# A fused attention and mixture-of-experts kernel: the query and key factors on VectorE, and the stack rows stored and loaded for all 512 tokens at once

## The chip, the cores and the metric

The kernel runs on one core of a Trainium2 chip. A core has TensorE (matrix products, and transposes as products with an identity matrix), VectorE, ScalarE and GpSimd for everything elementwise, and SyncE, which here only issues DMAs; the DMA engines move data between the chip's DRAM and the on-chip memory SBUF (128 partitions). Products are written to PSUM, eight banks of 2 KB per partition. In views of the profile the engines are PE (PEld for its loads of weights), DVE, ACT, POOL and SP. The metric is the device time of one execution in microseconds; lower is better.

## The reference

The input is 16 sequences of 512 tokens with 256 channels. Two blocks follow one another, each with a layer norm ahead of it and a residual around it:

```
x = x + attention_1(layernorm(x))      # 16 heads of 16, causal
x = x + ffn(layernorm(x))

attention_1:  q, k, v = x @ Wq.T, x @ Wk.T, x @ Wv.T, in 16 heads of 16
              q = layernorm(q, gq, bq);  k = layernorm(k, gk, bk)      # over the 16 channels of a head
              out = softmax(causal(q k^T)) v @ Wo.T + bo

ffn:          x = x + attention_2(rmsnorm(x))        # latent keys and values, rotary, 16 heads of 64
              x = x + moe(rmsnorm(x))                # 8 routed experts (top 2) and a shared one
```

`gq, bq, gk, bk` are the factors (gains) and offsets of the norm on queries and keys: the change moves their application. The rest of the reference is the same before and after.

## The kernel before

**Sequences and stages.** The program goes through the 16 sequences one after another. For each, TensorE does attention 1, attention 2 and the expert stage. In the expert stage a loop over steps e = 0 to 9 takes the shared expert and the eight routed ones: in step e TensorE does the up projections of expert e+1 (`gate_up`, L850) and the down projection of expert e-1 (`down`, L874), ScalarE the Silu (L1131) and the high half of the hidden values (`hidh`), VectorE the products with the gates and the rest `hidl` (L1474, L1479, L1483). `hid` of a step is wanted by TensorE one step later.

**What lies in between: the next sequence.** Its queries and keys are prepared during this expert stage, in four tiles of 128 tokens. For tile t: projection on TensorE (L681), the raw copy and the squares on ScalarE, the sums of squares on VectorE (`square_sums`), their root on GpSimd (`root_qk`, L559), the scaling on VectorE (`scale_qk`, L1271), factor and offset on GpSimd (`gains`, L564 and L565), four transposes on TensorE (`turn_qk`, L703, into bank 6 or 7). Then the float32 values are split into three bfloat16 parts, high, middle and low: ScalarE writes the high part (`high_part_qk`), VectorE the rest (`rest_qk`, L1277), ScalarE the middle part (`mid_part_qk`), VectorE the low part (`low_part_qk`, L1282). Four tables (L384 to L387) say in which step which tile is turned and split: turns in steps 2, 3, 5 and 6, the last part of the split of tiles 2 and 3 in step 7.

**Stash and stack.** Scores of attention 1 are one product over 96 rows per head: six slots of 16 rows hold the parts of the queries and of the keys in such pairs that the products add up to full precision (`QUERY_SLOTS`, `KEY_SLOTS`). A part lies in SBUF as 128 partitions x 4 x 512 tokens; SyncE stores it to DRAM (`stash`) and loads it back from there into each slot that wants it (`qkt`): a slot is 16 partitions, each with 16 heads. This is done in two halves of 256 tokens: per half three stores of 256 KB and twelve loads of 128 KB, in runs of 512 B. SyncE works strictly in its program order (`stack_rows`): high store, middle store, then a wait for the high store, six loads, low store, a wait for the middle store, four loads, a wait for the low store, two loads; then the second half.

**Who waits for that.** Tiles of attention are units u = 0 to 15 (four groups of four heads, tile j = u % 4, with (j+1) x 128 keys). `score` (L716 and the mask, L722) of unit 0 and 1 need only tokens of the first half, and wait for `stack_loaded[0]`; unit 2 waits for `stack_loaded[1]`. TensorE does the score of unit 0 of the next sequence ahead of the last down projection (the end of the expert loop). The parts share memory with `prob` and `probt`, so ScalarE's exp of unit 1 and TensorE's first transposes of probabilities (L733) wait until all parts are stored.

Of the kernel before, what the change touches and what calls it, by code (L numbers as in the profile page):

```python
# [98 lines left out]
def _build(nc, ctx, dram):  # L99
# [183 lines left out]
    high_stored = Signal(sem("high_stored"), 2 * 16)  # L283
    mid_stored = Signal(sem("mid_stored"), 2 * 16)
    low_stored = Signal(sem("low_stored"), 2 * 16)
    stack_loaded = [Signal(sem(f"stack_loaded{half}"), 2 * SPLITS * 16) for half in range(2)]
# [56 lines left out]
    DVE_LINKS, POOL_LINKS = 24, 7  # L343
# [59 lines left out]
    def _(sp):  # L403
# [57 lines left out]
        def load_slots(k, half):  # L461
            tokens = slice(half * 2 * P, (half + 1) * 2 * P)
# [5 lines left out]
        def stack_rows(b, half):  # L468
            if b > 0:
                sp.wait_ge(stack_loaded[half].sem, stack_loaded[half].at(b, 0))  # L470
            sp.wait_ge(high_ready.sem, high_ready.at(b, 2 * half + 2))
            store_part(0, half, high_stored)
            sp.wait_ge(mid_ready.sem, mid_ready.at(b, 2 * half + 2))
            store_part(1, half, mid_stored)
            sp.wait_ge(high_stored.sem, high_stored.at(b, 16 * (half + 1)))
            load_slots(0, half)
            sp.wait_ge(low_ready.sem, low_ready.at(b, 2 * half + 2))
            store_part(2, half, low_stored)
            sp.wait_ge(mid_stored.sem, mid_stored.at(b, 16 * (half + 1)))
            load_slots(1, half)  # L480
            sp.wait_ge(low_stored.sem, low_stored.at(b, 16 * (half + 1)))
            load_slots(2, half)

        for half in range(2):
            stack_rows(0, half)
        for b in range(NB - 1):
            sp.wait_ge(y_added.sem, y_added.at(b, NT))
            sp.dma_start(x_in[:, :, :], dram["x_rows"][bass.ds(b * L + L, L)].rearrange("(t p) c -> p t c", p=P)).then_inc(x_loaded.sem, 16)
            for half in range(2):
                stack_rows(b + 1, half)  # L490
# [8 lines left out]
    def _(pool):  # L499
        chain = Chain(pool, pool_link, POOL_LINKS, NT)  # L500
# [60 lines left out]
        def gains(b, t):  # L561
            pool.wait_ge(qn_ready.sem, qn_ready.at(b, t + 1))
            v = qn[:, t].rearrange("p (w h d) -> p w h d", w=2, h=H)
            chain.link(nc.gpsimd.tensor_tensor(v, v, gam[:, :, :].unsqueeze(2).to_broadcast([P, 2, H, D]), ALU.mult))  # L564
            nc.gpsimd.tensor_tensor(v, v, bet[:, :, :].unsqueeze(2).to_broadcast([P, 2, H, D]), ALU.add).then_inc(qhat_ready.sem, 1)  # L565

        def prepare(b):
            root_qk(b, 0)
            for t in range(NT):
                if t + 1 < NT:  # L570
                    root_qk(b, t + 1)
                if b > 0:
                    gains(b, t)
            for t in range(NT):
                nc.gpsimd.tensor_tensor(x_in[:, t], x_in[:, t], bo[:, :], ALU.add).then_inc(xb_ready.sem, 1)
# [50 lines left out]
    def _(pe):  # L626
# [129 lines left out]
        def attend(b, a, last):  # L756
# [3 lines left out]
            for u in range(UNITS):  # L760
# [3 lines left out]
                if u == 0:  # L764
                    if a == 0:
                        pe.wait_ge(down_added.sem, down_added.at(b, 0))
                        pe.wait_ge(rest_ready.sem, rest_ready.at(b, NT))
                        pe.wait_ge(high_stored.sem, high_stored.at(b, 32))
                        pe.wait_ge(mid_stored.sem, mid_stored.at(b, 32))
                        pe.wait_ge(low_stored.sem, low_stored.at(b, 32))  # L770
# [107 lines left out]
        def sequence(b, last):  # L878
# [56 lines left out]
            for e in range(NE + 1):  # L935
                if not last:
# [3 lines left out]
                    if e in TURN_FIRST:  # L940
                        turn_qk(b + 1, TURN_FIRST[e])
# [32 lines left out]
    def _(act):  # L974
# [37 lines left out]
        def high_part_qk(b, t):  # L1012
            act.wait_ge(qkt_psum.sem, qkt_psum.at(b, t + 1))
            if b > 0 and t % 2 == 0:
                act.wait_ge(high_stored.sem, high_stored.at(b - 1, 32))
# [6 lines left out]
        def exps(b, a, u, part):  # L1022
# [5 lines left out]
            if a == 0 and u == 1 and part == 0:  # L1028
                act.wait_ge(mid_stored.sem, mid_stored.at(b, 32))
                act.wait_ge(low_stored.sem, low_stored.at(b, 32))  # L1030
# [42 lines left out]
        def sequence(b, last):  # L1073
# [52 lines left out]
            for e in range(NE + 1):  # L1126
# [12 lines left out]
                if not last:  # L1139
                    if e in PROJECT_AT:  # L1140
                        copy_raw(b + 1, PROJECT_AT[e])
                    for t in MID_AT.get(e, ()):
                        mid_part_qk(b + 1, t)
                    for t in HIGH_AT.get(e, ()):
                        high_part_qk(b + 1, t)
# [32 lines left out]
    def _(dve):  # L1178
        chain = Chain(dve, dve_link, DVE_LINKS, 6)
# [50 lines left out]
        def first_gains(t):  # L1230
# [3 lines left out]
            dve.wait_ge(gained, t + 1)  # L1234
            tt(v, v, bet[:, :, :].unsqueeze(2).to_broadcast([P, 2, H, D]), ALU.add).then_inc(qhat_ready.sem, 1)
# [149 lines left out]
        def sequence(b, last):  # L1385
# [83 lines left out]
            for e in range(NE + 1):  # L1469
# [14 lines left out]
                if not last:  # L1484
                    for t in MID_AT.get(e, ()):
                        low_part_qk(b + 1, t)
# [109 lines left out]
```

## Time and profile before

| | |
|---|---|
| Three runs | 3693.62, 3697.82, 3698.3 us; median 3697.82 |
| Profiled execution | 3694.8 us, of which its span 3693.0 us |
| Mean granted TensorE clock | 0.965 of full |
| Busy: PE, DVE, ACT, POOL | 3270.5, 2721.6, 2138.6, 1116.0 us |
| Chain that ended last | PE 63%, ACT 12%, DMA 11%, DVE 7% |
| Stack loads, stash stores | 384 and 96, median 5.9 and 5.5 us from issue to landing |

One sequence takes some 226 us, and the same pattern returns in each. A view of the whole program therefore gives means over stages with different limits: where one stage is in question, a window of one sequence is read, here from 672 to 762 us, where the third seam between two sequences lies. Granted clock is that of TensorE, 1.00 for 2.4 GHz and 0.50 for 1.2 GHz.

### The profile page before, as it was taken

What the parts mean: (1) busy time and instruction counts of PE and PEld (TensorE: products, weight loads), DVE (VectorE), ACT (ScalarE), POOL (GpSimd) and SP (SyncE); (2) the same over time, 40 slices, a digit from 0 to 9 for tenths busy, and PEclk for the clock granted to TensorE, in tenths of its full rate; (3) what the DMA queues carried; (4) which work ended last, traced back from release to release, by engine and by line L of the source; (5) the groups of instructions that cost most, each with busy time, mean ns of one, the idle gap of its engine ahead of it and who ended that gap; (6) DMA issues with size and microseconds to landing.
All of it is one profiled execution on the core that took longest, in us unless ns stands there. A gap on an engine that the chain in (4) does not pass through costs nothing.

```text
span 3693.0 us, 78801 instructions
## 1 busy us (share of the span) xinstructions
PE 3270.5 (89%) x29800; PEld 2563.0 (69%) x29880; DVE 2721.6 (74%) x5760; ACT 2138.6 (58%) x6105; POOL 1116.0 (30%) x776
## 2 busy tenths in 40 slices
PE   4998989979899898988989899898998989989898
PEld 3676766857677676776767667676676766857676
DVE  5876867767777777767777687786876768767675
ACT  3655656556565565646656466564655646556564
POOL 3351242412324223242222423124241242412320
PEclk7999999999999999999999999999999999999999
DMA  6003040120402104030030300404003040120400
GB/s 132 7 12 53 2 58 7 25 40 2 58 7 38 27 2 58 7 50 15 1 58 7 58 7 2 58 7 58 7 11 55 2 58 7 23 42 2 58 1 7
DMA packets 188985, 104.24 MB, mean 28 GB/s; under 512 B 16640, under 2 KB 188544, under 8 KB 188608
## 3 DMA queue, kind: packets, MB, share of 16 engines
q1 hardware_dynamic: 188608, 99.21, 17.6%
q8 instruction: 238, 3.90, 0.5%
q14 instruction: 139, 1.14, 0.1%
HBM read 65.62 MB, written 33.55 MB: 27 GB/s over the span
## 4 chain that ended last, share of the span: by engine, by line
PE 63%; ACT 12%; DMA 11%; DVE 7%; issue 3%; SPq 3%; POOL 1%; ACTq 0%; POOLq 0%; DVEq 0%
PE bank L733 15%; PE bank L744 9%; DMA stash<-part 8%; PE scores L850 8%; ACT prob L1032 6%; PE scores L720 5%; PE scores L721 4%; PE scores L801 4%; SPq L466 3%; PE bank L681 3%; PE scores L824 3%; PE scores L722 3%; DMA qkt<-stash 3%; PE scores L716 2%; PE bank L874 2%
## 5 line engine op out<-in xcount | busy, mean ns | idle before, releaser
L1032 ACT ACTIVATE prob<-scores,negmax 128x128 f32<-128x128 f32 (+3 forms) x2048 | 1059.7, 536 | 396.2 <-DVE negmax L1293 285.7
L1293 DVE TENSOR_REDUCE negmax<-scores 128x1 f32<-128x128 f32 (+3 forms) x2048 | 873.1, 482 | 133.1 <-PE scores L722 118.9
L733 PE MATMUL bank<-ident,prob 128*128 128x128 f32 x5120 | 743.9, 283 | 143.3 <-DMA stash<-part 95.2
L1301 DVE COPY probt<-bank 128x512 f32<-128x512 f32 x896 | 596.5, 683 | 267.7 <-PE bank L733 261.7
L733 PEld LDWEIGHTS bank<-ident,prob 128*128 128x128 f32 x5120 | 558.9, 144 | 259.7 <-issue 168.8
L722 PE MATMUL scores<-mask,ident 128*128 128x128 bf16 x2048 | 445.5, 230 | 0.0
L1032 ACT ACTIVATION_READ_ACCUMULATOR prob<-scores,negmax 128x1 f32 x2048 | 434.8, 212 | 0.0
L720 PE MATMUL scores<-khh,qt 128*128 128x256 f32 (+2 forms) x1024 | 416.3, 407 | 13.3 <-POOL kll L610 13.3
L541 POOL COPY rexp<-rsum 128x512 f32<-128x512 f32 x128 | 78.3, 611 | 1053.2 <-DVE rsum L1305 1053.2
L546 POOL TENSOR_TENSOR otl<-onm,oth 128x512 fp32r<-128x512 f32 x96 | 122.8, 1279 | 882.8 <-ACT oth L977 882.8
L559 POOL TENSOR_TENSOR rq<-ssq,expo 128x32 f32<-128x32 f32 x64 | 359.8, 5633 | 48.0 <-DVE ssq L1265 48.0
L716 PE MATMUL scores<-qkt 96*128 96x128 bf16 (+3 forms) x1024 | 270.1, 322 | 104.4 <-DMA qkt<-stash 82.9
L977 ACT ACTIVATE probt<-bank 128x512 f32<-128x512 f32 x384 | 232.7, 606 | 209.0 <-PE bank L733 209.0
L850 PE MATMUL scores<-xth,wgu 128*128 128x512 f32 x1152 | 336.0, 413 | 1.3 <-ACT sg L1131 1.3
L721 PE MATMUL scores<-kll,qt 128*128 128x256 f32 (+2 forms) x1024 | 331.4, 324 | 0.0
L722 PEld LDWEIGHTS scores<-mask,ident 128*128 128x128 bf16 x2048 | 204.7, 100 | 136.2 <-issue 110.5
L1131 ACT ACTIVATE sg<-scores 128x512 f32<-128x512 f32 x144 | 85.7, 595 | 305.0 <-PE scores L850 304.8
L850 PEld LDWEIGHTS scores<-xth,wgu 128*128 128x128 f32 x1152 | 216.0, 190 | 42.0 <-issue 0.3
L874 PE MATMUL bank<-wd,hidh 128*128 128x256 f32 x1152 | 218.2, 289 | 29.7 <-DVE hidl L1479 29.7
L716 PEld LDWEIGHTS scores<-qkt 96*128 96x128 bf16 x1024 | 104.6, 102 | 199.3 <-DMA qkt<-stash 84.8
L720 PEld LDWEIGHTS scores<-khh,qt 128*128 128x128 f32 x1024 | 203.1, 198 | 18.8 <-POOL kll L610 17.1
L874 PEld LDWEIGHTS bank<-wd,hidh 128*128 128x128 f32 x1152 | 184.1, 193 | 40.1 <-ACT hidh L977 33.7
(185 smaller groups left out, 6236.9 us busy)
## 6 DMA issues: line engine op xcount, KB each, us to landing
qkt<-stash SPq DMA_DIRECT2D x384, 128.0 KB, 5.9
stash<-part SPq DMA_DIRECT2D x96, 256.0 KB, 5.5
x_in<-in_x_rows SPq DMA_DIRECT2D x16, 512.0 KB, 3.9
out_rows<-x SPq DMA_DIRECT2D x16, 512.0 KB, 6.5
r_d<-in_wd SPq DMA_DIRECT2D x1, 1024.0 KB, 8.1
r_gu<-in_wg SPq DMA_DIRECT2D x2, 512.0 KB, 4.6
r_gu<-in_wu SPq DMA_DIRECT2D x2, 512.0 KB, 5.7
r_wob<-in_wo SPq DMA_DIRECT2D x4, 128.0 KB, 5.2
```

The costliest lines, as they stand in the source:

```text
L559: nc.gpsimd.tensor_tensor(rq[:, s], ssq[:, s], expo[:, 0:1].to_broadcast([P, 2 * H]), ALU.pow).then_inc(rq_ready.sem, 1)
L716: mm(bank[q][:, 0:n], qkt[:, h, j * P:(j + 1) * P], qkt[:, H + h, 0:n], start=True, stop=False)
L720: mm(bank[q][:, 0:m], tok, khh[:, 0:m], start=True, stop=False)
L721: mm(bank[q][:, 0:m], tok, kll[:, 0:m], start=False, stop=False)
L722: ins = mm(bank[q][:, n - P:n], ident16[:, :], mask16[:, :], start=False, stop=True)
L733: ins = nc.tensor.transpose(bank[4 + n % 2][:, q * P:(q + 1) * P], prob[:, u % 2, q, i * P:(i + 1) * P], ident[:, :])
L744: ins = mm(bank[6][q * HP:(q + 1) * HP, j * P:(j + 1) * P], val, probt[:, u % 2, i, q * P:(q + 1) * P], start=i == 0, stop=i == j)
L850: ins = mm(bank[2 * s + w][:, :], wgu[:, w_, e, k, w * I:(w + 1) * I], XT[x_][:, k], start=m == 0 and k == 0, stop=m == 2 and k == KC - 1)
L874: ins = mm(bank[4 + t // 2][:, (t % 2) * C:(t % 2 + 1) * C], (hidh, hidl)[x_][:, s, t * P:(t + 1) * P], wd[:, w_, e], start=e == 0 and m = ...
L1032: nc.scalar.activation(prob[:, u % 2, q, 0:n], bank[q][:, 0:n], ACT.Exp, bias=negmax[:, a, u, q:q + 1], accum_out=sums[:, a, u, q:q + 1]). ...
L1293: nc.vector.tensor_reduce(negmax[:, a, u, M * part:M * part + M], scores[:, M * part:M * part + M, 0:n], axis=AX.X, op=ALU.max, negate=Tru ...
L1301: nc.vector.tensor_copy(probt[:, u % 2, i], bank[4 + n % 2][:, :]).then_inc(probt_dve.sem, 1)
```

## The change

Three things are done together.

1. `gains` is a function of VectorE now. Per tile it is two `tensor_tensor` operations of 128 x 512, factor and offset, right behind `scale_qk`. GpSimd keeps the four roots per sequence and the addition of `bo` to the next input.
2. Tiles are turned in steps 1, 2, 3 and 4 (`TURN_AT`) and split in steps 2, 3, 4 and 5 (`SPLIT_AT`), where one step has the high, rest, middle and low part of one tile.
3. There are no halves any more. A part is stored in one DMA of 512 KB once all four tiles have it, and a slot is loaded in one DMA of 256 KB, in runs of 1 KB: 15 DMAs per sequence in place of 30. There is one signal `stack_loaded`, and the score of unit 0 waits for it.

The core of the diff:

```diff
-    stack_loaded = [Signal(sem(f"stack_loaded{half}"), 2 * SPLITS * 16) for half in range(2)]
+    stack_loaded = Signal(sem("stack_loaded"), 2 * SPLITS * 16)
...
-    TURN_AT = {2: 0, 3: 1, 5: 2}
-    TURN_FIRST = {6: 3}
-    HIGH_AT = {3: (0,), 4: (1,), 6: (2, 3)}
-    MID_AT = {4: (0,), 5: (1,), 7: (2, 3)}
+    TURN_AT = {1: 0, 2: 1, 3: 2, 4: 3}
+    SPLIT_AT = {2: 0, 3: 1, 4: 2, 5: 3}
...
-        def store_part(k, half, signal):
-            tokens = slice(half * 2 * P, (half + 1) * 2 * P)
-            sp.dma_start(stash[k].rearrange("(c p) l -> p c l", p=P)[:, :, tokens], part[:, k, :, tokens]).then_inc(signal.sem, 16)
+        def store_part(k, signal):
+            sp.dma_start(stash[k].rearrange("(c p) l -> p c l", p=P), part[:, k]).then_inc(signal.sem, 16)
...
-                    sp.dma_start(qkt[s * D:(s + 1) * D, first:first + H, tokens], rows[:, :, tokens]).then_inc(stack_loaded[half].sem, 16)
+                    sp.dma_start(qkt[s * D:(s + 1) * D, first:first + H], rows).then_inc(stack_loaded.sem, 16)
...
-            sp.wait_ge(high_ready.sem, high_ready.at(b, 2 * half + 2))
+            sp.wait_ge(high_ready.sem, high_ready.at(b, NT))
...
-            if a == 0 and part == 0 and u in (0, 2):
-                pe.wait_ge(stack_loaded[u // 2].sem, stack_loaded[u // 2].at(b, 2 * SPLITS * 16))
+            if a == 0 and part == 0 and u == 0:
+                pe.wait_ge(stack_loaded.sem, stack_loaded.at(b, 2 * SPLITS * 16))
...
+        def gains(b, t):
+            dve.wait_ge(qn_ready.sem, qn_ready.at(b, t + 1))
+            v = qn[:, t].rearrange("p (w h d) -> p w h d", w=2, h=H)
+            chain.link(tt(v, v, gam[:, :, :].unsqueeze(2).to_broadcast([P, 2, H, D]), ALU.mult))
             tt(v, v, bet[:, :, :].unsqueeze(2).to_broadcast([P, 2, H, D]), ALU.add).then_inc(qhat_ready.sem, 1)
...
                     if e < 2:
-                        if e == 0:
-                            square_sums(b + 1, 2)
+                        square_sums(b + 1, e + 2)
+                    if e in SPLIT_AT:
+                        rest_qk(b + 1, SPLIT_AT[e])
+                    if e < NT:
                         scale_qk(b + 1, e)
-                        if e == 1:
-                            square_sums(b + 1, 3)
+                        gains(b + 1, e)
+                    if e in SPLIT_AT:
+                        low_part_qk(b + 1, SPLIT_AT[e])
```

How the instructions stand in a row, at three places. First SyncE, one whole sequence from the load of the next input (`x_in`) to the store of the output. Before:

```order
L488 DMA x_in<-in_x_rows 128x4x256
L459 DMA stash<-part 128x4x256 x2
L466 DMA qkt<-stash 16x16x256 x6
L459 DMA stash<-part 128x4x256
L466 DMA qkt<-stash 16x16x256 x6
L459 DMA stash<-part 128x4x256 x2
L466 DMA qkt<-stash 16x16x256 x6
L459 DMA stash<-part 128x4x256
L466 DMA qkt<-stash 16x16x256 x6
L492 DMA out_rows<-x_106 128x4x256
```

and now:

```order
L484 DMA x_in<-in_x_rows 128x4x256
L456 DMA stash<-part 128x4x512 x2
L462 DMA qkt<-stash 16x16x512 x6
L456 DMA stash<-part 128x4x512
L462 DMA qkt<-stash 16x16x512 x6
L487 DMA out_rows<-x_106 128x4x256
```

The two passes of stores and loads became one, with transfers twice as large; both of the first two stores now stand behind the last tile's high part.

Second ScalarE in the expert loop, steps 3 to 5 (one Silu, `sg<-scores`, opens each step; `part<-bank` is a high part, `part<-rest` a middle one). Before:

```order
L1131 ACTIVATE sg<-scores 128x512
L977 ACTIVATE hidh<-sg 128x512
L977 ACTIVATE part<-bank 128x4x128
L1131 ACTIVATE sg<-scores 128x512
L977 ACTIVATE hidh<-sg 128x512
L977 ACTIVATE part<-rest 128x4x128
L977 ACTIVATE part<-bank 128x4x128
L1131 ACTIVATE sg<-scores 128x512
L977 ACTIVATE hidh<-sg 128x512
L977 ACTIVATE part<-rest 128x4x128
```

and now, steps 4 and 5:

```order
L1114 ACTIVATE sg<-scores 128x512
L960 ACTIVATE hidh<-sg 128x512
L960 ACTIVATE part<-bank 128x4x128
L960 ACTIVATE part<-rest 128x4x128
L1114 ACTIVATE sg<-scores 128x512
L960 ACTIVATE hidh<-sg 128x512
L960 ACTIVATE part<-bank 128x4x128
L960 ACTIVATE part<-rest 128x4x128
```

High and middle part of a tile moved into the same step, and with step 5 the last tile is done.

Third VectorE in steps 3 and 4 (`rest<-bank` is the rest, `part<-rest` the low part, `qn<-qn,rq` the scaling). Before:

```order
L1474 TENSOR_TENSOR sg<-scores,sg 128x512
L1479 TENSOR_TENSOR hidl<-sg,hidh 128x512
L1483 TENSOR_TENSOR sg<-scores,sg 128x512
L1271 TENSOR_TENSOR qn<-qn,rq 128x512
L1277 TENSOR_TENSOR rest<-bank,part 128x512
L1474 TENSOR_TENSOR sg<-scores,sg 128x512
```

and now, step 3 and the beginning of step 4:

```order
L1462 TENSOR_TENSOR sg<-scores,sg 128x512
L1467 TENSOR_TENSOR hidl<-sg,hidh 128x512
L1471 TENSOR_TENSOR sg<-scores,sg 128x512
L1265 TENSOR_TENSOR rest<-bank,part 128x512
L1259 TENSOR_TENSOR qn<-qn,rq 128x512
L1222 TENSOR_TENSOR qn<-qn,gam 128x512
L1223 TENSOR_TENSOR qn<-qn,bet 128x512
L1270 TENSOR_TENSOR part<-rest,part 128x4x128
L1462 TENSOR_TENSOR sg<-scores,sg 128x512
```

Three operations moved into this step: the factor and the offset, which GpSimd had, and the low part, which stood one step later.

## Rows read from the trace of the kernel before

**Rows 1.** The page, its part 4: the chain that ended last, by engine.
```profile
PE 63%; ACT 12%; DMA 11%; DVE 7%; issue 3%; SPq 3%; POOL 1%; ACTq 0%; POOLq 0%; DVEq 0%
```
**Rows 2.** Waits: engine, line, awaited: total us, times, longest us.
```profile
PE bank L733 <- DMA stash<-part: 95.2, 16, 7.5
PE scores L716 <- DMA qkt<-stash: 82.9, 17, 5.5
```
**Rows 3.** Timeline of SyncE at one seam: start us, us, instruction.
```profile
720.72 4.67 SPq L459 DMA_DIRECT2D stash<-part  x2
725.44 3.04 SPq L466 DMA_DIRECT2D qkt<-stash  x6
```
**Rows 4.** Timeline of TensorE there; in brackets the idle time before, and what ended it.
```profile
718.33 0.60 PE L703 MATMUL bank<-ident,qn 128*128 128x128 f32 x4
718.68 0.48 PE L874 MATMUL bank<-wd,hidh 128*128 128x256 f32 x2
...
742.23 0.23 PE L716 MATMUL scores<-qkt 96*128 96x128 bf16 x1
...
742.75 0.47 PE L874 MATMUL bank<-wd,hidh 128*128 128x256 f32 x2
...
751.43 1.08 PE L733 MATMUL bank<-ident,prob 128*128 128x128 f32 x4 [6.33 <-DMA stash<-part]
757.72 0.50 PE L716 MATMUL scores<-qkt 96*128 96x384 bf16 x1 [5.21 <-DMA qkt<-stash]
...
766.29 0.22 PE L716 MATMUL scores<-qkt 96*128 96x128 bf16 x1
...
772.17 0.33 PE L716 MATMUL scores<-qkt 96*128 96x384 bf16 x1
...
779.20 0.22 PE L716 MATMUL scores<-qkt 96*128 96x128 bf16 x1
```
**Rows 5.** Windows: from:to, length, busy us by engine, granted clock, DMA share, GB/s.
```profile
729.50:733.30 3.80, 3.80 (x23) 3.25 (x22) 2.57 (x4) 0.92 (x2) 2.00 (x3) 1.00 1.25 116
735.00:740.40 5.40, 3.93 (x24) 3.17 (x22) 2.87 (x5) 2.65 (x4) 0.00 (x0) 1.00 1.24 132
745.50:749.10 3.60, 0.00 (x0) 0.00 (x0) 1.64 (x5) 0.00 (x0) 0.00 (x0) 1.00 1.24 113
...
28.00:32.00 4.00, 3.51 (x19) 2.82 (x18) 1.82 (x5) 1.36 (x3) 4.00 (x2) 1.00 1.20 296
721.60:722.20 0.60, 0.60 (x4) 0.52 (x3) 0.60 (x1) 0.00 (x0) 0.60 (x1) 1.00 0.90 268
...
757.70:763.00 5.30, 5.28 (x29) 3.38 (x30) 2.98 (x6) 2.96 (x9) 0.00 (x0) 0.51 0.06 19
```
**Rows 6.** DMA, 735 to 745 us: GB/s in 40 slices of 0.25 us.
```profile
GB/s 119 150 150 127 102 129 139 133 106 113 150 131 111 107 148 133 117 105 150 129 168 221 281 342 352 272 190 103 20 2 0 27 193 262 232 176 125 148 125 104
```
**Rows 7.** Timelines of VectorE, ScalarE and GpSimd in the same sequence.
```profile
705.77 1.67 DVE L1479 TENSOR_TENSOR hidl<-sg,hidh 128x512 fp32r<-128x512 f32 x1
...
710.59 0.68 DVE L1479 TENSOR_TENSOR hidl<-sg,hidh 128x512 fp32r<-128x512 f32 x1
...
744.44 1.29 DVE L1505 TENSOR_TENSOR x<-bank,x 128x512 f32<-128x512 f32 x2 [1.00 <-PE bank L874]
...
723.38 0.60 ACT L1131 ACTIVATE sg<-scores 128x512 f32<-128x512 f32 x1 [2.73 <-PE scores L850]
...
715.32 5.88 POOL L559 TENSOR_TENSOR rq<-ssq,expo 128x32 f32<-128x32 f32 x1
```
**Rows 8.** DMAs that run alone (720:724, and the end): issues, KB, us to landing.
```profile
stash<-part SPq DMA_DIRECT2D x1, 256.0 KB, 2.3
...
out_rows<-x SPq DMA_DIRECT2D x1, 512.0 KB, 3.0
```
**Rows 9.** Timelines of the first sequence: VectorE's last rest, TensorE's score of unit 2.
```profile
60.74 0.69 DVE L1277 TENSOR_TENSOR rest<-bank,part 128x512 f32<-128x512 f32 x1 [1.61 <-ACT part L977]
...
77.75 0.50 PE L716 MATMUL scores<-qkt 96*128 96x384 bf16 x1 [3.98 <-DMA qkt<-stash]
```

More of the change, by code:

```diff
@@ L342, in _build @@
     pool_link = sem("pool_link")
-    DVE_LINKS, POOL_LINKS = 24, 7
+    DVE_LINKS, POOL_LINKS = 28, 3
     block = ctx.enter_context(nc.Block())
@@ L455, in _, with load_slots @@
         sp.sem_inc(out_stored.sem, 16)
-        def store_part(k, half, signal):
-            tokens = slice(half * 2 * P, (half + 1) * 2 * P)
-            sp.dma_start(stash[k].rearrange("(c p) l -> p c l", p=P)[:, :, tokens], part[:, k, :, tokens]).then_inc(signal.sem, 16)
-        def load_slots(k, half):
-            tokens = slice(half * 2 * P, (half + 1) * 2 * P)
+        def store_part(k, signal):
+            sp.dma_start(stash[k].rearrange("(c p) l -> p c l", p=P), part[:, k]).then_inc(signal.sem, 16)
+        def load_slots(k):
             for first, slots in ((0, QUERY_SLOTS[k]), (H, KEY_SLOTS[k])):
@@ L465, in load_slots, with stack_rows @@
                 for s in slots:
-                    sp.dma_start(qkt[s * D:(s + 1) * D, first:first + H, tokens], rows[:, :, tokens]).then_inc(stack_loaded[half].sem, 16)
-        def stack_rows(b, half):
+                    sp.dma_start(qkt[s * D:(s + 1) * D, first:first + H], rows).then_inc(stack_loaded.sem, 16)
+        def stack_rows(b):
             if b > 0:
-                sp.wait_ge(stack_loaded[half].sem, stack_loaded[half].at(b, 0))
-            sp.wait_ge(high_ready.sem, high_ready.at(b, 2 * half + 2))
[L472 to L485, printed above, removed]
+                sp.wait_ge(stack_loaded.sem, stack_loaded.at(b, 0))
+            sp.wait_ge(high_ready.sem, high_ready.at(b, NT))
+            store_part(0, high_stored)
+            sp.wait_ge(mid_ready.sem, mid_ready.at(b, NT))
+            store_part(1, mid_stored)
+            sp.wait_ge(high_stored.sem, high_stored.at(b, 16))
+            load_slots(0)
+            sp.wait_ge(low_ready.sem, low_ready.at(b, NT))
+            store_part(2, low_stored)
+            sp.wait_ge(mid_stored.sem, mid_stored.at(b, 16))
+            load_slots(1)
+            sp.wait_ge(low_stored.sem, low_stored.at(b, 16))
+            load_slots(2)
+        stack_rows(0)
         for b in range(NB - 1):
@@ L488, in _ @@
             sp.dma_start(x_in[:, :, :], dram["x_rows"][bass.ds(b * L + L, L)].rearrange("(t p) c -> p t c", p=P)).then_inc(x_loaded.sem, 16)
-            for half in range(2):
-                stack_rows(b + 1, half)
+            stack_rows(b + 1)
             sp.wait_ge(down_added.sem, down_added.at(b, 1))
@@ L499, in _ @@
     def _(pool):
-        chain = Chain(pool, pool_link, POOL_LINKS, NT)
+        chain = Chain(pool, pool_link, POOL_LINKS, 0)
         nc.gpsimd.memset(expo[:, :], -0.5)
@@ L559, in root_qk @@
             nc.gpsimd.tensor_tensor(rq[:, s], ssq[:, s], expo[:, 0:1].to_broadcast([P, 2 * H]), ALU.pow).then_inc(rq_ready.sem, 1)
[L561 to L565, printed above, removed]
         def prepare(b):
-            root_qk(b, 0)
             for t in range(NT):
[L570 to L573, printed above, removed]
+                root_qk(b, t)
             for t in range(NT):
@@ L767, in attend @@
                         pe.wait_ge(rest_ready.sem, rest_ready.at(b, NT))
[L768 to L770 removed]
+                        pe.wait_ge(high_stored.sem, high_stored.at(b, 16))
+                        pe.wait_ge(mid_stored.sem, mid_stored.at(b, 16))
+                        pe.wait_ge(low_stored.sem, low_stored.at(b, 16))
                     else:
@@ L1141, in sequence @@
                         copy_raw(b + 1, PROJECT_AT[e])
[L1142 to L1145, printed above, removed]
+                    if e in SPLIT_AT:
+                        high_part_qk(b + 1, SPLIT_AT[e])
+                        mid_part_qk(b + 1, SPLIT_AT[e])
                 if e == 0:
@@ L1178, in _ @@
     def _(dve):
-        chain = Chain(dve, dve_link, DVE_LINKS, 6)
+        chain = Chain(dve, dve_link, DVE_LINKS, 6 + NT)
         tt, ts, stt = nc.vector.tensor_tensor, nc.vector.tensor_scalar, nc.vector.scalar_tensor_tensor
```

24 lines of the change are left out of this document (8 added, 16 removed).

## The prediction

> **What bounds the kernel now.** The page's chain of work that ended last is 63% TensorE, but 11% DMA [rows 1]. Eleven per cent of 3693 us is some 400 us of chain in transfers, so the list of waits came next, and TensorE's own waits there name two transfers: 95.2 us in 16 waits for the stores of the parts and 82.9 us in 17 waits for the loads of the stack rows [rows 2]. That is once per sequence of 16, at the seam where attention of the next sequence begins. Then I followed one seam (the third of 15, and those I looked at beside it are alike to 0.1 us) on SyncE and on TensorE. SyncE issues the first stores at 720.72 and the first loads at 725.44 [rows 3]. TensorE comes to the score of unit 0 at 742.23, does the last down projection and the score of unit 1, and has been out of work for 6.33 us when it gets 4 transposes in at 751.43, the low part having left; the score of unit 2 starts only at 757.72, when the second half of the rows is in [rows 4]. So a seam is bound by DMA, and what the change is worth is decided by when the *last* stack row lands, and by what TensorE can do before that.
>
> **What sets the pace of the loads.** Where only stack loads move, the DMA engines are full and pass 116, 132 and 113 GB/s in three stretches [rows 5], mean 120. Their packets are 512 B, and each load fills 16 partitions. The expert weights at the start are 512 B packets as well, into 128 partitions, and run at 296 GB/s; the stash stores, 512 B out of 128 partitions, at 268 [rows 5]. So the size of a packet isn't what holds the loads at 120; what differs is the 16 partitions, or else the source's pattern (512 B out of each 1 KB row). A second sign: a group of loads begins with 193, 262, 232, 176 GB/s for a microsecond and goes on at 125 and less [rows 6], as if reads ran ahead until the writing side was full. I take it that bytes at the 16 partitions are the limit, which the change leaves as it is. The trace has no stretch of 1 KB packets into 16 partitions alone, so the price is bounded: 132 to 113 GB/s if bytes limit, 240 if each packet costs the same. I take 120.
> The Trainium skill, "SBUF — State Buffer", section "Door 1: The DMA port swizzle", says that bits of the partition number pick one of 16 ports; 16 partitions in a row then reach 4 ports, a quarter of about 436 GB/s, an estimate of 109. The rows lie a little above it. By 109 in place of 120 each set of rows would land 2.7 us later and the sum below would be 3853.
>
> **The change, part by part, on the clock of this seam.**
> (1) Factors and offsets go from GpSimd to VectorE: 8 more instructions per sequence of the 128x512 form that takes 0.68 us, of which 0.6 shows [rows 7]: 4.8 us. Against them, VectorE's instruction of that form takes 1.67 us where GpSimd works on the factors beside it [rows 7]; six such in this seam give back some 4 us together. The rest is covered: in steps 2 and 3 of the expert loop VectorE has 8 operations, 4.9 us, in steps of 4.4 to 4.8, and falls behind by under 1 us, while TensorE takes what VectorE made in step 3 (ready by 716) only at 718.68 [rows 4]. If that cover of 2.8 us went, each microsecond would cost 15. Priced at 0.
> (2) Turns in steps 1, 2, 3, 4 in place of 2, 3, 5, 6: the same 4 transposes each, 0.35 us of TensorE (718.33 to 718.68 [rows 4]), none added. Each needs the offsets from VectorE's step before, some 3 us ahead of the turn: 0. GpSimd's roots take 5.88 us each [rows 7]; without the factors between them the last one runs from 710 to 716, and the scaling that needs it comes at 717: 0, with 1 us of cover on a side that has 2.8 behind it.
> (3) Splits, one tile in each of steps 2 to 5, high and middle part together: ScalarE waits about 1 us between the two for VectorE's rest, in the gap that it has before each Silu (2.73 us [rows 7]): 0. The Silu of step 5 starts at 723.38; a third turn ahead of it makes that 723.7. Two more operations of 0.5, and the high part of the last tile is being stored from 725.3; the middle part is ready at 727.3, the low one at 728.
> (4) The DMA chain. A store of 512 KB in 1 KB packets lands in 3.0 us when alone, one of 256 KB in 2.3 [rows 8]; that is 1.4 us for the data of 512 KB and 1.6 fixed. First load issued at 728.4; the middle store's data is out of its way at 730.1. Then 12 loads of 256 KB, 3.146 MB, at 120 GB/s: 26.2 us; the low store in between, 1.4; the last row lands 1.6 after its data: 730.1 + 26.2 + 1.4 + 1.6 = **759.3**. Before, it was in at 757.7. Half as many issues save nothing, since the DMA engines are full behind them; and no load can start before the last tile is split.
> (5) What waits for it. TensorE now waits at unit 0's score, from 742.2 on, for *all* rows. Behind that wait stand the last down projection (so VectorE's last additions), the score of unit 1 and the first transposes, all done under the transfer before. From 759.3: four scores 0.95 (0.52 from 742.23 to 742.75 at full clock), down projection 3.0 (1.6, from 742.75 [rows 4] to the addition that waits for it at 744.44 [rows 7]; twice about, as the clock is down), additions 1.3 [rows 7], first maximum and exp 0.95: 6.2, so unit 2 at 765.5. After the wait the granted clock is 0.51, the lower level, for 5.3 us [rows 5]. Before, that fell on units 2 and 3: 8.57 us from the score of unit 2 to that of unit 4, where the next group takes 7.03 [rows 4]. After, it falls on those 6.2 us. Unit 4: 765.5 + 7.0 = 772.5 against 766.3, **+6.2 us per seam**, 93 us for 15. By 132 GB/s it is +3.8 (57 us), by 113 +7.8 (117 us).
> (6) The first sequence. The last tile's parts come at 60.74 [rows 9], the loads' data flow from 64.4 on; 64.4 + 26.2 + 3.0 = 93.6, unit 2 4.5 later (no down projection here), unit 4 at 105.1, against 77.75 [rows 9] + 8.57 = 86.3: +19 (16 to 20).
>
> Sum: 93 + 19 = 112. On the profiled execution, 3694.8 us, that gives 3806.8; it lies 3 us under the median of the runs, 3697.8, on which it is **3810 us**. By the ends of the rate, 3697.8 + 57 + 16 = 3771 and 3697.8 + 117 + 20 = 3835.
>
> **Rivals.**
> *A, a packet costs the same whatever its size.* Loads at 240 GB/s take 13.1 us, the last row is in at 746.2, a wait of 4 us. Unit 2 at +4.6 = 750.8, unit 4 at 757.8, 8.5 us earlier than now; 127 us for 15, less 6 in the first sequence: 3577. For it: the source is then read in whole rows. Against it: 296 beside 120 at one packet size, and the burst. Slower turns into faster at 163 GB/s (19.3 us of loads); from 132 to there the time is 3771 to 3698.
> The Trainium skill, "DMA: Bandwidth & Descriptors", section "Measured", has larger DMAs nearer to peak, 138 GB/s at 64 KB and 341 at 1 MB, which speaks for this rival; the stack loads at 128 KB lie under the curve it gives, by the rows.
> *B, larger loads overlap less.* The series falls to 105 to 111 inside a group and rises to 130 to 150 again and again [rows 6], perhaps where two loads meet that fill different partitions. Loads twice as long meet half as often: 105 GB/s, 30 us, +10 per seam and +23 at the start, 3870.
> *C, the seam is as I say, but a step lags too.* Should ScalarE's wait in (3) or VectorE's lag in (1) reach TensorE with 2 us per sequence, it is 30 us on top: 3840.
>
> **How the numbers follow.** Forecast, 3771 to 3835: 0.52. B and C together 0.17. Between 132 and 163 GB/s 0.12, of which 0.02 lies within 0.2% of no change (7 us, about what a measurement of this kernel can tell). A and what lies on its side 0.19. The range leaves out A and the farthest of B: from 3720, in the middle of the half-way case, to 3865. Faster 0.19, same 0.02, slower 0.79.
>
> **What the profile after would show.** Stack loads at about 120 GB/s and packets of 1 KB; TensorE idle once per seam, for about 17 us, ended by the stack rows at a score of 128 columns, with no wait for the stores of the parts any more; the down projection behind it; the high store issued about 4.6 us later than now, at 725. I am wrong if the loads run above 163 GB/s (A), if a turn waits for VectorE, or if TensorE shows new idle time in steps 1 to 6.

## The result, and the profile after

The changed kernel takes 3813.3 us (median of 4 runs, 3813.1 to 3814.6), the kernel before 3697.3 (4 runs beside them): 1.0316 times as long, 95% interval 1.0298 to 1.0334. It is **116 us slower**, against 112 forecast. The profiled execution has a span of 3811.3 us at a mean granted clock of 0.953 (before 3693.0 at 0.965).

The page of the kernel after: busy time by engine, the DMA queue (packets, MB, share of 16 engines), the chain that ended last by engine, and two lines of DMA issues (count, KB each, median us from issue to landing).

```profile
PE 3267.3 (86%) x29880; PEld 2558.9 (67%) x29880; DVE 2739.5 (72%) x5880; ACT 2138.7 (56%) x6105; POOL 945.5 (25%) x656
...
q1 hardware_dynamic: 111040, 99.19, 16.6%
...
PE 56%; DMA 13%; DVE 13%; ACT 12%; issue 4%; SPq 2%; POOL 1%; ACTq 0%; POOLq 0%; DVEq 0%
...
qkt<-stash SPq DMA_DIRECT2D x192, 256.0 KB, 12.3
stash<-part SPq DMA_DIRECT2D x48, 512.0 KB, 3.5
```

No engine has much more to do: TensorE is busy for 3267 us where it was 3270, VectorE for 18 us more. What grew is the chain's part in transfers, 11% [rows 1] to 13%, and in VectorE, 7% to 13%. The waits say where (engine, line, awaited: total us, times, longest us):

```profile
PE scores L701 <- DMA qkt<-stash: 286.0, 16, 35.3
...
ACT part L960 <- DVE rest L1265: 132.8, 63, 3.3
```

TensorE waits for stack rows 286 us where it waited 83, and its 95 us for the stores of the parts are gone [rows 2]. Without the first sequence that is (286.0 - 35.3) / 15 = 16.7 us per seam. The second line is ScalarE's wait for VectorE's rests, which no step of the sum had at that size. What it and VectorE's larger part in the chain are worth is taken up with steps (1) and (3) below.

The same seam as in the prediction follows (timelines: start us, us, instruction, idle time before and what ended it). Take 32.08 off these times to get the clock of the prediction: the last but one down projection, behind a wait of 1.84 us, starts at 740.76 before and at 772.84 now. SyncE first:

```profile
757.75 2.61 SPq L456 DMA_DIRECT2D stash<-part  x2
760.67 3.33 SPq L462 DMA_DIRECT2D qkt<-stash  x6
764.04 0.45 SPq L456 DMA_DIRECT2D stash<-part  x1
764.53 14.92 SPq L462 DMA_DIRECT2D qkt<-stash  x6
```

TensorE there:

```profile
772.84 0.47 PE L859 MATMUL bank<-wd,hidh 128*128 128x256 f32 x2 [1.84 <-DVE hidl L1467]
...
791.85 0.26 PE L701 MATMUL scores<-qkt 96*128 96x128 bf16 x1 [17.36 <-DMA qkt<-stash]
...
792.62 0.77 PE L859 MATMUL bank<-wd,hidh 128*128 128x256 f32 x2
...
795.31 0.28 PE L701 MATMUL scores<-qkt 96*128 96x256 bf16 x1
...
797.91 0.34 PE L701 MATMUL scores<-qkt 96*128 96x384 bf16 x1 [0.40 <-ACT prob L1015]
...
804.99 0.22 PE L701 MATMUL scores<-qkt 96*128 96x128 bf16 x1
```

On the clock of the prediction: high store at 725.7, first load at 728.6, the score of unit 0 at 759.8 (all rows in), unit 2 at 765.8, unit 4 at 772.9, where before it was 766.29 [rows 4]. In three windows (length, busy us by engine, granted clock, DMA share, GB/s):

```profile
763.50:769.50 6.00, 6.00 (x35) 5.17 (x34) 1.89 (x3) 1.19 (x3) 0.00 (x0) 1.00 1.16 113
780.00:788.00 8.00, 0.00 (x0) 0.00 (x0) 0.00 (x0) 0.00 (x0) 0.00 (x0) 0.50 1.17 119
792.00:795.00 3.00, 3.00 (x19) 3.00 (x18) 0.93 (x4) 1.51 (x8) 0.00 (x0) 0.50 0.00 0
```

The loads move 113 and 119 GB/s in packets of 1 KB, where the packets of 512 B moved 113 to 132 [rows 5]; in the second window TensorE does nothing for 8 us; in the third it is back, at the lower clock, with work that used to lie under the transfer.

### The profile page after: what moved, and what is told of

Its sections match the earlier page's. It is cut to its first block, busy times and chain, and to the rows that moved or that the text cites. A ratio compares the mean times of both kernels' runs of the same rounds, so it can differ in the third digit from the quotient of the medians.

```text
span 3811.3 us, 78610 instructions
## 1 busy us (share of the span) xinstructions
PE 3267.3 (86%) x29880; PEld 2558.9 (67%) x29880; DVE 2739.5 (72%) x5880; ACT 2138.7 (56%) x6105; POOL 945.5 (25%) x656
## 4 chain that ended last, share of the span: by engine, by line
PE 56%; DMA 13%; DVE 13%; ACT 12%; issue 4%; SPq 2%; POOL 1%; ACTq 0%; POOLq 0%; DVEq 0%
PE bank L718 13%; PE bank L729 8%; DMA stash<-part 7%; ACT prob L1015 6%; PE scores L705 5%; DMA qkt<-stash 5%; PE scores L786 4%; PE scores L706 4%; PE scores L835 4%; PE scores L809 3%; PE scores L707 3%; PE bank L666 2%; DVE negmax L1281 2%; PE bank L859 2%; PE scores L701 2%
## 5 line engine op out<-in xcount | busy, mean ns | idle before, releaser
L718 PE MATMUL bank<-ident,prob 128*128 128x128 f32 x5120 | 726.3, 279 | 56.5 <-DVE probt L1289 43.4
L718 PEld LDWEIGHTS bank<-ident,prob 128*128 128x128 f32 x5120 | 544.6, 141 | 171.0 <-issue 66.6
L701 PE MATMUL scores<-qkt 96*128 96x128 bf16 (+3 forms) x1024 | 265.9, 313 | 312.9 <-DMA qkt<-stash 286.0
L859 PE MATMUL bank<-wd,hidh 128*128 128x256 f32 x1152 | 236.7, 305 | 29.7 <-DVE hidl L1467 29.7
L859 PEld LDWEIGHTS bank<-wd,hidh 128*128 128x128 f32 x1152 | 197.4, 208 | 38.6 <-ACT hidh L960 33.7
L706 PEld LDWEIGHTS scores<-kll,qt 128*128 128x128 f32 x1024 | 196.5, 192 | 0.0
```

Source lines behind the costliest of these rows:

```text
L701: mm(bank[q][:, 0:n], qkt[:, h, j * P:(j + 1) * P], qkt[:, H + h, 0:n], start=True, stop=False)
L706: mm(bank[q][:, 0:m], tok, kll[:, 0:m], start=False, stop=False)
L718: ins = nc.tensor.transpose(bank[4 + n % 2][:, q * P:(q + 1) * P], prob[:, u % 2, q, i * P:(i + 1) * P], ident[:, :])
L859: ins = mm(bank[4 + t // 2][:, (t % 2) * C:(t % 2 + 1) * C], (hidh, hidl)[x_][:, s, t * P:(t + 1) * P], wd[:, w_, e], start=e == 0 and m = ...
```

## Experiments: which part does what

The theory: (i) bytes at the 16 partitions that a load fills set its pace; (ii) loading all tokens at once costs, since no load can start before the last tile is split, and unit 0 waits for all; (iii) earlier turns and splits gain; (iv) factors on VectorE cost nothing. The change is taken apart first. All expectations are for the whole program; a ratio is to the kernel before, with its 95% interval. Each kernel was timed beside the kernel before on the same chip.

**whole_late.** The kernel before, with part 3 of the change alone: parts stored and slots loaded whole.

```diff
-                    sp.dma_start(qkt[s * D:(s + 1) * D, first:first + H, tokens], rows[:, :, tokens]).then_inc(stack_loaded[half].sem, 16)
+                    sp.dma_start(qkt[s * D:(s + 1) * D, first:first + H], rows).then_inc(stack_loaded.sem, 16)
```

> The kernel before with part 3 alone: whole parts stored, slots loaded for 512 tokens, one signal; turns, splits and GpSimd's factors as before. Theory: the middle part of the last tile comes at 735.1, the loads' data flow from about 737.2 on, so 737.2 + 26.2 + 3.0 = 766.4 for the last row, 7 us later than in the changed kernel: 3900 to 3930 us. Were the change's loss due to VectorE's new work, this would be near 3697.

Measured: 3915.6 us, ratio 1.0597 (1.0579 to 1.0614), as expected. TensorE's line of waits:

```profile
PE scores L713 <- DMA qkt<-stash: 387.9, 16, 33.5
```

**halves_early.** The changed kernel with part 3 undone: factors on VectorE and the early turns and splits, with halves.

```diff
-            sp.wait_ge(high_ready.sem, high_ready.at(b, NT))
-            store_part(0, high_stored)
+            sp.wait_ge(high_ready.sem, high_ready.at(b, 2 * half + 2))
+            store_part(0, half, high_stored)
...
-            if a == 0 and part == 0 and u == 0:
+            if a == 0 and part == 0 and u in (0, 2):
```

> The changed kernel with part 3 undone: two halves, 30 DMAs in runs of 512 B, two signals, as before; factors on VectorE and the early turns and splits stay. Theory (loads limited in bytes, all at 120 GB/s; the loss comes from waiting for the last tile and from the work that stands behind the one signal): the DMA chain runs as before but starts about 4.4 us earlier, unit 2 about 4.4 to 6 us earlier per seam than before: 3610 to 3640 us. If parts 1 and 2 carried a loss of their own, it would be above that, and above 3697 if they carried most of it.

Measured: 3604.3 us, 0.9752 (0.9737 to 0.9766), 6 us under the range I expected. SyncE's timeline at the same seam (add 12.56 for the clock of the prediction):

```profile
703.21 3.20 SPq L457 DMA_DIRECT2D stash<-part  x2
706.46 3.06 SPq L464 DMA_DIRECT2D qkt<-stash  x6
709.56 0.45 SPq L457 DMA_DIRECT2D stash<-part  x1
710.05 8.20 SPq L464 DMA_DIRECT2D qkt<-stash  x6
```

TensorE's scores of units 2 and 4 there:

```profile
738.78 0.50 PE L704 MATMUL scores<-qkt 96*128 96x384 bf16 x1 [4.93 <-DMA qkt<-stash]
...
747.35 0.22 PE L704 MATMUL scores<-qkt 96*128 96x128 bf16 x1
```

Its line of waits:

```profile
PE scores L704 <- DMA qkt<-stash: 74.7, 17, 5.4
```

The first stores leave at 715.8 in place of 720.72, the first loads at 719.0 in place of 725.44 [rows 3], and unit 2 starts at 751.3 in place of 757.72 [rows 4]: 6.4 us, 96 for 15 seams, where 92 are measured. The wait for the stores [rows 2] is gone but for one of 4.7 us.

So the result is the balance of two opposite effects. Against about 3697 us: the early steps (with the factors on VectorE) alone -92, the whole transfers alone +219, both +116. They don't add up exactly: with whole transfers the early steps are worth 3916 - 3813 = 102 us.

Going from halves to whole costs 3813 - 3604 = 209 us, 13.1 per sequence, and the two timelines show what it consists of. The last tile's high part is written at the same time in both, 725.0 on the clock of the prediction. But with halves the first load leaves at 719.0 and all rows are in at 751.3; with whole parts it leaves at 728.6 and the rows are in at 759.8, 8.4 us later. From there to the score of unit 4 it takes 8.6 us with halves and 13.1 with whole parts, since the down projection, the score of unit 1 and the first transposes now stand behind the wait: 4.6 us more. Together that is 13.0 us per seam.

**gains_only.** The kernel before, with `gains` on VectorE alone.

```diff
-            chain.link(nc.gpsimd.tensor_tensor(v, v, gam[:, :, :].unsqueeze(2).to_broadcast([P, 2, H, D]), ALU.mult))
+            chain.link(tt(v, v, gam[:, :, :].unsqueeze(2).to_broadcast([P, 2, H, D]), ALU.mult))
```

> The kernel before with part 1 alone: factors and offsets by VectorE, right behind the scaling of each tile, GpSimd keeps the roots; turns, splits, halves as before. Theory: covered, and every part still reaches SyncE when it did: 3697 us within 8. Rival C of the prediction (VectorE's lag reaches TensorE): 3710 to 3730.

Measured over 11 runs: 3692.6 us, ratio 1.0000 (0.9991 to 1.0008), no change within 3 us. Busy times by engine in this kernel:

```profile
PE 3270.1 (89%) x29800; PEld 2562.1 (69%) x29880; DVE 2744.7 (74%) x5880; ACT 2137.9 (58%) x6105; POOL 952.1 (26%) x656
```

TensorE's two waits for transfers there:

```profile
PE bank L723 <- DMA stash<-part: 91.6, 16, 6.7
PE scores L706 <- DMA qkt<-stash: 85.4, 17, 5.6
```

GpSimd loses 164 of its 1116 us, VectorE is busy only 23 us longer though it has 120 instructions more, and the two waits of the seam are nearly the ones it had [rows 2]. So where the turns and splits stay late, both effects lie off the path. Whether the early steps could be had with the factors still on GpSimd was not tried.

## Experiments: what limits the loads

**whole_spread6.** The changed kernel with slot s in rows s, s + 6, s + 12, ... of the stack in place of 16 in a row. Scores add over all 96 rows, in whatever order they stand. Bytes, packets, issues and waits stay the same; only where a load's 16 rows land changes.

```diff
-                    sp.dma_start(qkt[s * D:(s + 1) * D, first:first + H], rows).then_inc(stack_loaded.sem, 16)
+                    sp.dma_start(qkt[s:SD:SPLITS, first:first + H], rows).then_inc(stack_loaded.sem, 16)
```

> The changed kernel with one edit: the 16 rows of slot s lie on partitions s, s+6, ..., s+90 and no longer on 16 partitions in a row. Packets (1 KB), bytes, number of partitions per load (16), source and order are the same; the products over 96 rows add up the same pairs. Theory (the writing side is limited by which partitions a load fills): stack loads at 250 to 330 GB/s where they ran at 105 to 120, the last row in some 2 us after TensorE comes to the score of unit 0 (742.2 on the clock of the seam in the prediction), TensorE's wait there 0 to 3 us in place of 17.4, and 3530 to 3570 us. Rival (the source's pattern in DRAM, or the issue of descriptors, limits the loads): no change of rate, 3813 us.

Measured: 3608.6 us, 0.9764 (0.9750 to 0.9779). Windows at the seam (only stack loads move in the first three; the third and fourth lie on either side of TensorE's wait):

```profile
725.50:729.50 4.00, 4.00 (x24) 3.47 (x25) 1.89 (x3) 1.12 (x2) 0.00 (x0) 1.00 1.14 218
728.50:731.00 2.50, 2.50 (x13) 2.03 (x13) 0.69 (x2) 0.00 (x0) 0.00 (x0) 1.00 1.14 229
...
735.00:736.50 1.50, 1.50 (x10) 1.39 (x8) 0.69 (x1) 0.57 (x1) 0.00 (x0) 0.58 1.12 229
...
740.00:744.00 4.00, 3.88 (x23) 3.76 (x24) 1.09 (x5) 1.51 (x8) 0.00 (x0) 0.50 0.00 0
```

TensorE's wait in between:

```profile
740.12 0.27 PE L701 MATMUL scores<-qkt 96*128 96x128 bf16 x1 [3.43 <-DMA qkt<-stash]
```

One slice in the code nearly doubles the rate, 113 to 119 becoming 218 to 229 GB/s, and takes 205 us off the changed kernel. The same 1 KB packets from the same source go twice as fast into rows that lie apart, so neither the packet nor the source's pattern held them; only the place where the rows land differs. That corrects (i) as well: each load still fills 16 partitions with the same bytes each, so it isn't the bytes per partition that set the pace, but that the 16 lie in a row. The size I expected was wrong: 3530 to 3570 us from 250 to 330 GB/s, where the expert weights have 296 into 128 partitions [rows 5]. The rate stops near 222 GB/s. By it 3.146 MB take 14.2 us against some 27 at 113 to 119, 12.9 us per sequence less; the times give 12.8.

**whole_spread2.** Two slots share 32 rows, one the even and one the odd rows.

```diff
+                    sp.dma_start(qkt[s // 2 * 2 * D + s % 2:(s // 2 + 1) * 2 * D:2, first:first + H], rows).then_inc(stack_loaded.sem, 16)
```

> As whole_spread6, but two slots share 32 partitions in a row, every second one each, so that a load's 16 rows reach 8 groups of 4 partitions where the changed kernel's reach 4. Theory, as a matter of degree: if groups of partitions are what is shared, the rate doubles to 210 to 240 GB/s, the last row lands at about 747 to 749 on the seam's clock, a wait of 5 us, and the time is 3580 to 3620 us, between 3813 and whole_spread6. Rival (any spreading helps alike, say since neighbouring partitions collide): the same as whole_spread6. Rival (source limits): 3813.

Measured: 3630.1 us, 0.9825 (0.9811 to 0.9840); two windows of loads alone, one among the first six of the seam, one among the last six:

```profile
728.50:733.00 4.50, 4.50 (x26) 3.88 (x27) 1.89 (x3) 1.12 (x2) 0.00 (x0) 1.00 1.14 190
737.50:741.00 3.50, 1.65 (x12) 1.48 (x12) 1.32 (x3) 0.63 (x1) 0.00 (x0) 1.00 1.13 217
```

Twice as many rows are spanned, and the rate of the first loads is 1.6 to 1.7 times that of 16 in a row; the last ones run at 217. The time misses what I expected (3580 to 3620 us), and so does the rate of the first loads (210 to 240 GB/s), on the same side.

**whole_spread4.** Is it the span of rows that counts, or how many ways into the memory they reach? Four slots share 64 rows, every fourth each; the last two share 32.

```diff
+                    sp.dma_start(qkt[s:4 * D:4, first:first + H] if s < 4 else qkt[4 * D + s - 4:SD:2, first:first + H], rows).then_inc(stack_loaded.sem, 16)
```

> The changed kernel with slots 0 to 3 on every fourth partition of the first 64 and slots 4 and 5 on every second one of the last 32. It asks what 'spread' means. The first five loads of a sequence go to slots 0 to 3, each with one row in every group of 4 neighbours. Theory X (partitions p and p+32 share a way in, as the Trainium skill, 'SBUF — State Buffer', section 'Door 1: The DMA port swizzle', states): 16 rows then fall on 8 ways, 2 each, as in whole_spread2, and these five loads run at 186 to 200 GB/s like there. Theory Y (only the group of 4 neighbours is shared): 16 ways, and they run at 250 GB/s or more. Time by X 3600 to 3635 us, by Y 3560 to 3600.

Measured: 3627.4 us, 0.9814 (0.9797 to 0.9830); the same two windows:

```profile
728.50:733.00 4.50, 4.50 (x27) 3.93 (x26) 1.89 (x3) 1.12 (x2) 0.00 (x0) 1.00 1.14 202
737.00:741.00 4.00, 1.65 (x12) 1.48 (x12) 1.29 (x2) 0.63 (x1) 0.00 (x0) 1.00 1.15 217
```

A span of 64 rows gives almost what one of 32 gives (202 and 190 GB/s, then 217 and 217; the times differ by 0.1%, inside both intervals), and it stays far from 250.
The Trainium skill, "SBUF — State Buffer", section "Door 1: The DMA port swizzle", lets partition p and p + 32 share a port; by it these loads reach 8 ports at either span, 16 rows in a row reach 4, and every sixth of 96 rows reaches 13 or 14. The rates of the first loads (113, 190 to 202, 218 to 229 GB/s) rise in that order. An estimate from the Trainium skill's figures is 109 GB/s for 4 ports, 218 for 8 and 354 for 13; the rows lie a little above the first, at or below the second and far below the third, so the number of ports alone doesn't explain the last step.
By the Trainium skill's port map, though, two of the 16 rows of every sixth fall on one port at two or three of the ports. If a load goes at the pace of its fullest port, the same estimate is 218 GB/s for both spreads, near the 217 and 229 that the last six loads show. This would make the number of rows per port the limit throughout; it isn't shown, since no run changed that number while the ports stayed the same. It also leaves open why the first loads of the 8-port kernels lag behind (190 and 202): five of those six fill the same 8 ports by the Trainium skill's port map, while of the last six three go to each of two sets. No run tried 16 rows that lie apart and yet share 4 ports, so adjacency itself isn't excluded by a run of its own.

## Experiments: what stands behind the wait

Step 5 of the prediction puts 6.2 us of displaced work behind the wait, partly since it runs at the lower clock. Two variants of the changed kernel take one of these away.

**down_first.** The last down projection and VectorE's additions stand ahead of the wait for the stack rows.

```diff
-                if e == NE and not last:
-                    pe.wait_ge(hid_ready.sem, hid_ready.at(b, NE))
-                    for part in range(NM):
-                        score(b + 1, 0, 0, part)
...
                     down(b, e - 1)
+                if e == NE and not last:
+                    pe.wait_ge(hid_ready.sem, hid_ready.at(b, NE))
+                    for part in range(NM):
+                        score(b + 1, 0, 0, part)
```

> The changed kernel, but TensorE does the last down projection ahead of the score of unit 0, and VectorE its last additions ahead of the maxima of unit 0, so that this work no longer stands behind the wait for the stack rows. Step 5 of the prediction prices it at 3.0 us (down projection at the lower clock) and 1.3 (additions), of which the maxima and exp of unit 0 cover about 1.5 on the way to unit 1: 2.5 to 3 us per seam, 3813 becomes 3765 to 3780 us. If what stands behind the wait cost nothing, 3813.

Measured: 3783.9 us, 1.0244 (1.0229 to 1.0260), 4 us above the range I expected. TensorE's scores of units 0, 2 and 4:

```profile
788.10 0.26 PE L701 MATMUL scores<-qkt 96*128 96x128 bf16 x1 [13.94 <-DMA qkt<-stash]
...
791.67 0.53 PE L701 MATMUL scores<-qkt 96*128 96x384 bf16 x1
...
799.36 0.22 PE L701 MATMUL scores<-qkt 96*128 96x128 bf16 x1
```

From unit 0 to unit 2 it is 3.57 us in place of 6.06, so the displaced work was worth 2.5. But from unit 2 to unit 4 it is 7.69 in place of 7.08: the score of unit 2 lasts 0.53 in place of 0.34 us, as the lower clock, which fell on the down projection, now falls on it. Together that is 11.26 against 13.14, 1.9 us per seam: 28 us for 15, and 27 to 29 are measured (by the ratios and by the times).

**warm_wait.** The changed kernel, with 80 products that nobody reads ahead of the score of unit 0, to fill the wait.

```diff
+                    pe.wait_ge(rest_ready.sem, rest_ready.at(b + 1, NT))
+                    keep_busy(80, 6)
                     for part in range(NM):
                         score(b + 1, 0, 0, part)
```

> The changed kernel, with 80 products of 128x512 into a free bank ahead of the score of unit 0, about 17 us of work for TensorE that nobody reads, in place of most of the idle wait. Theory (step 5: after the wait the granted clock is at the lower level for some 5 us, and the scores, the last down projection and the score of unit 1 run at it): the clock stays at 1.00, unit 4 comes 1.5 to 2.5 us earlier per seam, 3813 becomes 3775 to 3795 us. If the clock made no part of the loss, 3813 or, since the products end a little late, up to 3825.

Measured: 3793.6 us, 1.0265 (1.0248 to 1.0282). The span and clock of the whole program:

```profile
core 0: 3793.0 us, clock 0.990
```

TensorE's scores of units 0 and 2:

```profile
789.67 0.23 PE L701 MATMUL scores<-qkt 96*128 96x128 bf16 x1
...
794.19 0.34 PE L701 MATMUL scores<-qkt 96*128 96x384 bf16 x1 [0.40 <-ACT prob L1017]
```

At the upper clock the same work takes 4.52 us in place of 6.06. So the clock is 1.5 us of each seam, 23 us in all by this seam, 19 by the ratios of the two kernels. Set against the kernel before, the 6.6 us that unit 4 comes later at this seam are 2.0 us of later landing of the last row (759.8 for 757.7) and 4.6 us between that and unit 4 (13.14 for 8.57). Each variant alone gives back less than half of the 4.6; the two together were not tried.

## Experiments: a version that beats both

**before_spread6.** The kernel before, with only the rows interleaved: `qkt[s:SD:SPLITS, first:first + H, tokens]` in the load.

> The kernel before with the rows of a slot on every sixth partition (s, s+6, ..., s+90), nothing else. Theory: loads at about 220 GB/s as in whole_spread6; the second half's stores still come at 735 to 737 on the seam's clock, its rows land at about 747, when TensorE has just come to unit 2; the seam loses nearly all of its 11.5 us of waiting and the time is 3520 to 3560 us. If packets of 512 B have a cost of their own once the partitions are spread, loads stay under 180 GB/s and the time is 3570 to 3610.

Measured: 3522.4 us, 0.9536 (0.9523 to 0.9550). SyncE's timeline at the seam, one group of loads:

```profile
714.28 3.83 SPq L466 DMA_DIRECT2D qkt<-stash  x6
```

TensorE's wait for stack rows in this kernel:

```profile
PE scores L716 <- DMA qkt<-stash: 16.7, 11, 3.3
```

**halves_early_spread6.** halves_early with the same slice.

> Parts 1 and 2 of the change, halves and two signals as before, and the rows of a slot on every sixth partition. Theory: last parts at 725 to 728, second half's rows in by 740 on the seam's clock, before TensorE asks for them; no wait for a transfer at the seam at all, unit 4 at 753.8, 12.5 us earlier than before: 3500 to 3530 us, faster than both kernels and than halves_early (3604). If a third limit stands behind the transfers (ScalarE's exp or VectorE's maxima at the seam), 3530 to 3560.

Measured: 3516.8 us, 0.9524 (0.9511 to 0.9537). The stack loads there:

```profile
qkt<-stash SPq DMA_DIRECT2D x384, 128.0 KB, 2.7
```

This has the lowest time here, 4.8% below the kernel before and 7.7% below the changed one by their ratios; before_spread6 lies 0.1% behind it, which the intervals don't tell apart. A load lands 2.7 us after its issue, where it took 5.9 before. TensorE's wait for stack rows falls from 82.9 us [rows 2] to 16.7 in before_spread6 and to a single one of 2.5 in halves_early_spread6, and with no long wait left the mean clock is 0.99 in both. Early turns and splits, worth 92 us with slow loads, are now worth about 6, which the noise doesn't tell from nothing: both gains were for the same wait. Whole transfers, though, cost 92 us even with spread rows (whole_spread6 at 3608.6 against 3516.8).

## Why the prediction was right

Taken by its steps, on the clock of the prediction:

- **Pace of the loads.** Taken 120 GB/s, bounds 113 to 132; the rows show 113 to 119, at twice the size of packet and load. The price was right, its reason only in part: whole_spread6 shows that the bytes at 16 partitions hold a load at this rate only where the 16 lie in a row. Rival A (a packet costs the same) is excluded: it needed over 163. So is B as a mean: it needed 105.
The Trainium skill, "DMA: Bandwidth & Descriptors", section "Measured", which made larger transfers faster, didn't decide here: its series is for 128 partitions, and at 16 in a row a doubling of the size changed nothing.
- **(1) Factors on VectorE, priced 0.** gains_only confirms the price where turns and splits are late; where they are early, the sum below closes without a term for it. The lag was mis-sized: under 1 us forecast, but in step 4 the Silu of ScalarE starts at 751.02 and VectorE's product with it only at 753.04, 2.0 us behind, where before it was 0.6; the lag is 1.4 us. ScalarE's timeline in the kernel after:

```profile
751.02 0.60 ACT L1114 ACTIVATE sg<-scores 128x512 f32<-128x512 f32 x1 [0.35 <-PE scores L835]
...
755.56 0.63 ACT L960 ACTIVATE part<-rest 128x512 bf16<-128x512 f32 x1 [2.93 <-DVE rest L1265]
756.10 0.58 ACT L1114 ACTIVATE sg<-scores 128x512 f32<-128x512 f32 x1
```

VectorE's there, and TensorE's down projection that takes this `hidl`:

```profile
753.04 0.68 DVE L1462 TENSOR_TENSOR sg<-scores,sg 128x512 f32<-128x512 f32 x1
753.64 0.68 DVE L1467 TENSOR_TENSOR hidl<-sg,hidh 128x512 fp32r<-128x512 f32 x1
...
755.99 0.48 PE L859 MATMUL bank<-wd,hidh 128*128 128x256 f32 x2
```

The lag hadn't reached TensorE by the end of the stage, where the wait for VectorE is 1.84 us in both kernels. The cover of 2.8 us held: `hidl` is ready at 754.32, and 1.7 us of cover are left.
- **(2) Turns, 0.** No turn waited. The early steps are part of what halves_early gains.
- **(3) Splits.** ScalarE's wait between high and middle part was put at about 1 us. It is 1.7 to 2.9 in this sequence, 132.8 in the program. The Silu of step 5 comes straight behind the late middle part, at 756.10 or 724.0 for 723.7, and its scores had been ready since 755.8. So VectorE is on the way to the high store now, which is what its 13% of the chain says, but it ends only 0.3 us after TensorE there, and the price of 0 nearly stands. Little cover is left: a VectorE that lags 2 us more would delay the stores, as rival C feared.
- **(4) The DMA chain.** High store 725.7 for 725.3, first load 728.6 for 728.4, all rows in at 759.8 for 759.3. The sum of 26.2 + 1.4 + 1.6 us held to 0.5 us.
- **(5) Behind the wait.** From score 0 to unit 2, 6.06 us for 6.2; unit 4 at 772.9 for 772.5, +6.6 us per seam for +6.2. Of the 6.06 us, the displaced work is 2.5 (down_first) and the lower clock 1.5 (warm_wait); the two overlap, since part of that work runs at the lower clock. The upper clock comes back between 795.0 and 795.5 (that window shows 0.74), so the scores, the down projection and no more ran at the lower one.
- **(6) The first sequence.** Unit 4 at 104.18, against 86.32 before: +17.9 us for +19.
- **Sum.** 15 x 6.6 + 17.9 = 117 us, for 112 forecast and 116 measured (118 between the two spans). Two errors of 6 and 1 us went opposite ways; neither is large, so the agreement isn't luck.

What the prediction lacked is that its +112 is the difference of two larger effects, -92 and +209 as measured. It followed one seam by the clock, which gives the difference directly, and so never priced the early steps alone. Nor did it draw from its own reading of the 16 partitions that spreading the rows would be the better change; the runs had to show that.

## What to carry to other kernels

Where DMA engines are full and yet slow, look at which partitions each transfer fills: 16 rows in a row moved 120 GB/s, the same rows interleaved over 96 moved 220, for one slice in the code. Making a transfer larger moves its start to the end of the work that fills it, and puts behind its wait what could run under the second half; here that cost 8.4 and 4.6 us per seam, and the larger transfers moved no faster to pay for it. When two edits are made at once, time each alone: here a gain of 92 us was hidden under a loss of some 210.

## What the runs showed of the hardware beyond what I expected

- Loads into 16 interleaved rows stop at 218 to 229 GB/s, where the weights into 128 partitions run at 296 [rows 5]. In before_spread6 SyncE takes 0.64 us to issue each load of 128 KB, 205 GB/s, so issuing may be the limit there; whole_spread6 takes 0.65 us for each of 256 KB, 400 GB/s, so there it isn't. Whether it is the fullest port, as estimated above, or something else stays open.
- The granted clock can fall while TensorE works, after a short pause. In whole_spread6 TensorE waits 1.84 us for VectorE, works on, and the window from 735.0 to 736.5 shows 0.58 on the average, ahead of the wait for the rows. After the same pause the changed kernel shows 1.00 up to 778.0, idle again since 774.5. What tells the two apart wasn't tried.
- Where GpSimd has no factors to do, most of VectorE's slowed products are gone (1.67 us [rows 7], now 0.68 for the same one; one of 1.10 is left in that sequence): 120 instructions more, at 0.6 us visible each 72 us, cost VectorE only 18 to 23 us of busy time. By gains_only that is worth nothing in time.
